# Issuing the next pair's scores at the end of the slot in every slot of the attention chain

## The reference, cut to what matters

```
q = (layernorm(x) @ Wq + bq)   k = ctx @ Wk + bk   v = ctx @ Wv + bv
attn = softmax(q_h . k_h * HEAD_DIM ** -0.5)       for 16 heads h
x = x + concat_h(attn @ v_h) @ Wo + bo
x = x + experts(layernorm(x))                      8 experts, the best 2 of each row
```

## Time and profile before

| | |
|---|---|
| median of three runs | 2083.99 us |
| the profiled execution | 2078.15 us |
| its span | 2075.3 us |
| mean granted TensorE clock | 0.922 of full |
| TensorE busy | 1774.3 us, 85% |
| VectorE busy | 1292.3 us, 62% |
| ScalarE busy | 930.4 us, 45% |
| GpSimd busy | 780.3 us, 38% |

### The profile page before, as it was taken

The page is one execution under the profiler, slowest core; times in us unless marked ns, Lnnn a source line. Parts: engine busy times, 40 slices in busy tenths (PEclk is TensorE's granted clock), DMA queues, the critical chain, the costliest instruction groups (busy, mean ns, idle before and its releaser), DMA issues.

```text
span 2075.3 us, 35354 instructions
## 1 busy us (share of the span) xinstructions
PE 1774.3 (85%) x10807; PEld 1367.3 (66%) x10807; DVE 1292.3 (62%) x3531; ACT 930.4 (45%) x3214; POOL 780.3 (38%) x803
## 2 busy tenths in 40 slices
PE   2999999999999997988788899988899968787864
PEld 1677767777677797755566678766688845464663
DVE  2467777676777543456656767666666756666643
ACT  1222222232222232677665545566554557677622
POOL 2354546466465413212423220243221143343345
PEclk7899999899999999999888999989899979888977
DMA  6505014321420497532100739100548344351756
GB/s 152 217 5 207 21 63 139 108 105 37 113 75 28 143 332 259 165 116 68 29 21 15 255 117 326 49 25 19 206 130 300 101 130 120 105 137 53 202 178 202
DMA packets 168280, 263.23 MB, mean 127 GB/s; under 512 B 24028, under 2 KB 101534, under 8 KB 167838
## 3 DMA queue, kind: packets, MB, share of 16 engines
q1 hardware_dynamic: 145870, 231.26, 34.6%
q0 software_dynamic: 12288, 25.19, 4.1%
q10 hardware_dynamic: 9936, 4.53, 0.8%
HBM read 196.48 MB, written 82.46 MB: 134 GB/s over the span
## 4 chain that ended last, share of the span: by engine, by line
PE 39%; DVE 12%; ACT 10%; issue 5%; DMA 3%; SPq 2%; POOL 1%; ACTq 0%; DVEq 0%; POOLq 0%
PE Y L1063 7%; PE up L1045 7%; ACT prob L1232 5%; PE B L862 3%; PE up L978 3%; PE A L854 3%; PE up L1050 3%; PE D L872 2%; DMA wg<-list 2%; ACT probT L1238 2%; DVE nmax L1429 2%; ACT kbd L1220 2%; PE Y L987 1%; PE up L854 1%; PE Y L1015 1%
## 5 line engine op out<-in xcount | busy, mean ns | idle before, releaser
L1881 POOL DMA_INDIRECT list<-xn,pos x192 | 191.9, 1000 | 371.0 <-DVE pos L1578 194.6
L1951 POOL TENSOR_TENSOR hid<-tg,uc 128x512 f32<-128x512 f32 x168 | 217.8, 1297 | 230.4 <-DVE tg L1667 229.1
L1238 ACT ACTIVATE probT<-B 128x512 f32<-128x512 f32 x256 | 157.5, 615 | 252.9 <-PE B L862 252.5
L1286 ACT ACTIVATE tg<-up 128x512 f32<-128x512 f32 x168 | 100.3, 597 | 299.1 <-PE up L978 286.4
L987 PEld LDWEIGHTS Y<-wd,hid 128*128 128x128 f32 x1344 | 180.4, 196 | 72.9 <-issue 45.1
L1232 ACT ACTIVATE prob<-up,nmax 128x128 f32<-128x128 f32 x596 | 212.6, 391 | 3.7 <-DVE nmax L1429 3.7
L1664 DVE TENSOR_TENSOR uc<-up,ytmp 128x512 f32<-128x512 f32 x168 | 115.0, 685 | 147.1 <-PE up L978 130.3
L978 PE MATMUL up<-x2T,wg 128*128 128x512 f32 x336 | 199.8, 677 | 2.7 <-DVE tg L1667 2.7
L862 PEld LDWEIGHTS B<-const,prob 128*128 128x128 f32 x1024 | 125.6, 152 | 111.9 <-issue 105.3
L1771 DVE COPY xsT<-Y 128x128 f32<-128x128 f32 x255 | 73.4, 288 | 200.7 <-PE Y L1015 196.4
L862 PE MATMUL B<-const,prob 128*128 128x128 f32 x1024 | 174.8, 297 | 16.8 <-ACT probT L1238 16.2
(11 more groups left out here) (241 smaller groups left out, 3785.7 us busy)
## 6 DMA issues: line engine op xcount, KB each, us to landing
w_tile<-wt SPq DMA_DIRECT2D x43, 768.0 KB, 6.7
list<-w_tile SPq DMA_DIRECT2D x21, 1536.0 KB, 14.2
w_tile<-wt SPq DMA_DIRECT2D x45, 512.0 KB, 4.9
w_tile<-wt SPq DMA_DIRECT2D x55, 321.0 KB, 3.8
wg<-list SPq DMA_DIRECT2D x255, 64.0 KB, 3.8
wd<-wt SPq DMA_DIRECT2D x18, 768.0 KB, 6.1
list<-wu SPq DMA_DIRECT2D x186, 64.0 KB
wd<-wt SPq DMA_DIRECT2D x16, 512.0 KB, 5.0
```

Source lines behind the costliest of these rows:

```text
L1238: act.activation(probT[:, (2 * r + i) % 4, :, :], B4[:, :, :], ACT.Copy).then_inc(probT_done.sem, 1)
L1881: pool.indirect_dma_start(out=list_to(K, g)[:, :], in_=xn2[:, t, :], in_offset=None, out_offset=bass.IndirectOffsetOnAxis(ap=pos[:, g, s, ...
L1951: pool.tensor_tensor(hid[:, n % HRING, :], tg[:, n % 2, :], uc[:, n % 2, :], ALU.mult)\
```

## The change

`early(S)` now holds wherever pair S and pair S-1 both exist, that is for S = 1 to 127. So the scores of the slots 24 to 88 are issued one slot sooner too, ahead of the tail of the slot before. The waits within `scores`, the banks and the other engines' programs are as before.

```diff
-                early = lambda S: S in THREE and S - 1 in THREE
+                early = lambda S: around(S)[0] and around(S - 1)[0]
                 if now and not early(S):
                     scores(*now, r)
```

## The result

The changed kernel took 2063.97 us (median of 4 runs, 2060.14 to 2068.6), the kernel before 2084.27 us in the same comparison (4 runs, 2079.95 to 2092.08). The ratio is 0.9899, 95% interval 0.9863 to 0.9936: about 20 us less. Two later comparisons of the same kernel gave 0.9908 and 0.9904. The forecast was 2059 us. It was added up as 22 us of gain, taken off 2081 us, the middle between the profiled execution before and the median; from the median of 2084 us it is 25 us.

The account below looks back on a forecast made before the run. TensorE was busiest (85% of the span), the bound changing by stage, with idle time mostly in light stretches. Order 13.7 us plus clock 8 us, about 22 us, gave 2056 or 2062 us by base; forecast 2059 us, range 2038 to 2082.

Parts of the forecast that it names:

- The place: Most of the gain lies in the light slots, where TensorE idles some 55 us, against 23 us in the routed.
- the light stretches: Slots 24 to 41 and 56 to 73, one shared tile per slot: each shrinks by 8 to 12 us.
- The routed stretches: Slots 42 to 55 and 74 to 87: VectorE's earlier start gains 5.0 us, later key projections lose 4.2 us.
- the wait for tg: Four routed slots behind a key projection: L1045 waits longer for VectorE's tg, 1.05 us lost each.
- Even and odd slots: Light slots: scores start before values or output projection; 0.47 and 0.23 us in examples, 7.0 and 1.4 us in all.
- scores for "ACT prob": Sign: new waits of the score matmuls on ScalarE's exponentials, 0.5 to 1 us each, in most light slots.
- The key projections: Four light slots: 3.8 us from idling filled, 2.7 us from VectorE sooner, 2.9 us lost to late key blocks.
- The transposed rows: Four light slots waiting 2.1 to 3.6 us for xn: the whole 1.05 us fits in each, 4.2 us.
- The losses: Slots 41, 56, 57, 73: little or no gap, early scores can hold up the tail; 3.3 us lost in all.
- The sum without the clock: All gains and losses of order in slots 24 to 88: 13.7 us, bounds 6 and 24 us.
- The clock: Light stretches: fewer drops of TensorE to 1.2 GHz behind long waits; 8 us, ends minus 8 and 27 us.
- The rival "slower": Key blocks' lateness on ScalarE stays over three slots of each of eight groups: 2091 us in all; chance 0.08.

Follow-up runs that it names:

- e2: Changed kernel with scores early only for the light-slot pairs 24 to 42 and 57 to 74: 2063.05 us, ratio 0.9894 to the kernel before.
- e7: Changed kernel with the key projection ahead of the early scores in the four routed slots that have one: 2050.54 us, ratio 0.9850.
- e12: Kernel before, TensorE's order untouched; in light slots ScalarE evacuates the second transposes ahead of the second quad's exponentials: 2069.44 us, ratio 0.9936.
- e9: The changed kernel run once more, unaltered, as anchor for later runs: 2060.76 us, ratio 0.9904 to the kernel before.
- e5: Kernel before, order untouched, with 67 idle matmuls put into TensorE's waits in the light slots: 2067.14 us, ratio 0.9938.
- e6: Changed kernel with 56 idle matmuls ahead of the early scores, within their waits in the light slots: 2046.83 us, ratio 0.9832.
- e8: Changed kernel without the five pairs 24, 42, 57, 58, 74, projection first in routed slots, idle matmuls within waits: 2040.62 us, ratio 0.9808.
- e1: The changed kernel run again, unaltered, as anchor: 2062.67 us, ratio 0.9908 to the kernel before.
- e4: Changed kernel without early scores for the five pairs 24, 42, 57, 58, 74: 2057.79 us, ratio 0.9871.
- e10: Changed kernel without the five pairs 24, 42, 57, 58, 74 and with projection first in routed slots, no idle matmuls: 2042.23 us, ratio 0.9829.
- e11: Changed kernel with the key projection ahead of the scores in all eight slots that have one, light and routed: 2049.76 us, ratio 0.9852.

## Why the prediction was right, point by point

*The total and the direction* were right: 22 us forecast, 20 us measured, within the range. The absolute time was forecast 5 us too low, 3 us of them through the base from which the gain was taken.

*The place* was right: e2 has all of the gain. How it lies in the light stretches was not foretold: each was to shrink by 8 to 12 us, and they shrank by 12.6 and 3.9 us. VectorE's waits for the scores were to vanish nearly there; a third and a half of them stayed.

*The routed stretches* were to gain 5.0 - 4.2 = 0.8 us. Both terms were there (e7 took the second away: 5.0 us, 4.2 predicted), and slots 46, 54, 78 and 86 have the wait for tg that was named. What the sum lacked is the longer wait for tile rows in slots 48 and 80, about 1.1 us each at the least. In two profiles without a drop of the clock there, the two stretches take 346.5 us with the scores at the head (e12) and 349.3 us with early ones (e9), so the order costs some 3 us. That the profile after shows no loss is luck: the one before had the low clock in slots 45 and 80.

*Even and odd slots.* Slot 32 went from 7.16 to 6.67 us, slot 34 from 7.20 to 6.68, slot 33 from 7.14 to 6.75: 0.5 and 0.4 us, where 0.47 and 0.23 stood. The wait that takes the others' place is the one named, scores for "ACT prob", 0.6 to 1.5 us in most light slots.

*The key projections* came near their sum: 3.8 + 2.7 - 2.9 us over four of them is 0.9 us each, and slot 37 at the full clock went from 9.37 us (e5) to 8.44 (e6). The parts are not borne out one by one, for the slot behind shows no loss to late key blocks: slot 38 went from 7.18 to 6.69 us, like other even slots. The transposed rows were mis-sized: slots 35 and 67 went from 8.22 to 7.60 us, 0.62 us each and not 1.05.

*The losses* had their size: 1.05, 1.05, 0.7 and 0.5 us for slots 41, 56, 57 and 73, 3.3 us in all, where e6 and e8 show 0.94, 0.99, 0.40 and 0.94 us, 3.3 us. In the profile after, slot 56 is 3.2 us longer and slot 57 is 0.7 us, because the episode of the low clock that was feared there came with it.

*The sum without the clock*: 12.9 us of the 13.7 fell to the light stretches, and the slots show some 14 us there (at most 15.6); less 3 us in the routed ones, that is 11 us. With some 9 us of clock it makes the 20 us measured, all of these being estimates.

*The clock* is the term that is least certain. I had 8 us; the profiles give 1 to 11 us, and the granted clock of all executions some 9 us. The episodes behind the long waits did go, as slot 37's rows show, but others came, behind slot 56 and in slots 30, 38 and 62 after waits of 1.5 us; the prediction had only the first of these. The rule that I weighed and gave less room (the Trainium skill, "TensorE: Matmul & The Clock Gate", section "A second HAM failure mode: psum-queue depth-cycling"), short idling between groups makes the clock swing, describes the new episodes, and in the second light stretch the clock is 0.90 after 0.91. In the first it rose from 0.87 to 0.93, which the rule alone would not give. By that rule my sum would have been 13.7 us, by the rows' reading 22, and slots 24 to 88 show 17.3, 18.2 and 22.9 us in three profiles.

*Slots 23 and 24* were not on my list; slot 23 is 2.0 us longer in the profile after. In e1 and e6 it is 0.7 us longer, with a wait of 0.8 us or less: the rest was the clock. Slot 24 gains 0.6 us in these two.

*The rival "slower"* (ScalarE's lateness over three slots) is excluded: slots 47 and 55 are 12.1 and 8.4 us, 0.1 us longer than before.

## What to carry to other kernels

In an in-order queue an instruction may be moved ahead of a wait as long as its own wait ends sooner than that one; list, slot by slot, both ends, and leave the few out in which it ends later (e4, e8, e10). Look one engine further too: a producer that is pushed back by 1 us costs that much where its consumer's queue is full, and little where it isn't (e7, e11). Look for waits on a DMA as well: an engine that comes to such a wait sooner does not get the data sooner (slots 48 and 80). And price idle time of TensorE twice, once as time and once as clock, the second only after an experiment that fills the waits, and from more than one profile.

## What the runs showed of the hardware

Matmuls that do nothing made a kernel faster: 67 of about 0.5 us each, set into waits of TensorE, took 13 us off the kernel before (e5) by the ratio, and 56 (e6) brought the granted clock of the changed kernel's light stretches from 0.93 and 0.90 to 0.99 and 1.00, and their length from 142.3 and 143.3 to 134.5 and 135.6 us. In the changed kernel the lower clock, 1.2 GHz, came back behind waits of 1.54 us in slots 30, 38 and 62, with waits of 0.6 us in the slots before: I had expected it behind longer waits alone. The length of a wait does not decide it, for in slots 25, 27 and 70 waits of 1.52, 1.97 and 1.54 us passed at 2.4 GHz.
